# Half a batch's projections, squares, roots and unit vectors moved within the last rounds of FFN 1

## The reference, cut to what matters

```
x = x + 0.5 * ffn(layernorm(x))            # FFN 1: hidden 384, silu(gate) * up, down
x = x + attention(layernorm(x))            # attention: x + gate * out @ Wo
x = x + 0.5 * ffn(layernorm(x))            # FFN 2

# attention(x):
h = rmsnorm(x) * norm_w
q = l2norm(h @ Wq)    # 4 heads of 32
k = l2norm(h @ Wk)    # 2 heads of 32
v = h @ Wv
out = softmax(causal(q @ k.T * exp(log_temperature))) @ v
```

## Time and profile before

| | us |
|---|---|
| median of 3 runs | 430.47 (430.47 to 430.57) |
| profiled execution | 430.8 |
| its span | 429.0 |
| PE busy | 393.1 (92%) |
| ACT busy | 370.0 (86%) |
| DVE busy | 349.1 (81%) |
| POOL busy | 299.7 (70%) |
| granted clock of TensorE, mean | 0.999 |

### The profile page before, as it was taken

The page is one execution under the profiler, slowest core; times in us unless marked ns, Lnnn a source line. Parts: engine busy times, 40 slices in busy tenths (PEclk is TensorE's granted clock), DMA queues, the critical chain, the costliest instruction groups (busy, mean ns, idle before and its releaser), DMA issues.

```text
span 429.0 us, 13351 instructions
## 1 busy us (share of the span) xinstructions
PE 393.1 (92%) x5403; PEld 219.8 (51%) x5403; DVE 349.1 (81%) x887; ACT 370.0 (86%) x497; POOL 299.7 (70%) x381
## 2 busy tenths in 40 slices
PE   0689999898898899999999999999999999999994
PEld 0346666574444434635546446456354346765754
DVE  4889999689596997997998979968769848878554
ACT  4799999776797698999998998999987989999950
POOL 5689999985799858857758578581123658999850
PEclk9999999999999999999999999999999999999999
DMA  6487523513605706418237148055142225566532
GB/s 171 102 194 156 67 49 50 99 27 76 124 2 76 125 2 127 74 16 143 46 75 101 26 76 128 2 107 93 20 87 46 39 38 75 111 136 100 126 96 79
DMA packets 119233, 35.25 MB, mean 82 GB/s; under 512 B 101632, under 2 KB 119168, under 8 KB 119168
## 3 DMA queue, kind: packets, MB, share of 16 engines
q1 hardware_dynamic: 117888, 34.02, 43.1%
q10 hardware_dynamic: 1280, 0.33, 0.3%
HBM read 4.98 MB, written 4.19 MB: 21 GB/s over the span
## 4 chain that ended last, share of the span: by engine, by line
PE 55%; DVE 13%; ACT 10%; DMA 8%; issue 6%; POOL 6%; SPq 1%; DVEq 0%; ACTq 0%
PE ps L740 11%; PE ps L770 10%; PE ps L777 10%; PE ps L511 9%; DMA QKT<-ST 5%; ACT XN L463 3%; PE ps L804 3%; PE ps L575 3%; PE ps L564 3%; DVE H L332 3%; ACT PT L884 3%; PE ps L600 3%; DVE RD L245 2%; PE ps L747 2%; DMA XT<-w_int 2%
## 5 line engine op out<-in xcount | busy, mean ns | idle before, releaser
L884 ACT ACTIVATE PT<-ps,k_exp 128x1024 f32<-128x1024 f32 x144 | 153.9, 1122 | 14.1 <-PE ps L747 8.0
L511 PE MATMUL ps<-XT,WT 128*128 128x512 f16 x384 | 93.9, 383 | 6.2 <-DVE H L332 2.0
L740 PE MATMUL ps<-QKT 128*32 128x512 f16 (+1 forms) x1280 | 86.6, 359 | 5.0 <-DMA QKT<-ST 3.3
L770 PE MATMUL ps<-PT,V 128*32 128x512 f32 (+3 forms) x768 | 76.1, 486 | 0.0
L777 PE MATMUL ps<-PT,ones 128*32 128x512 f32 (+3 forms) x768 | 76.1, 486 | 0.0
L438 POOL TENSOR_TENSOR HL<-H,HH 128x1024 f16<-128x1024 f32 x31 | 66.6, 2148 | 8.3 <-ACT HH L487 5.3
L332 DVE SCALAR_TENSOR_TENSOR H<-SG,k_isilu,ps 128x1536 f32<-128x1536 f32 x32 | 57.9, 1808 | 13.9 <-ACT SG L481 6.3
L511 PEld LDWEIGHTS ps<-XT,WT 128*128 128x128 f16 x384 | 34.5, 98 | 50.6 <-issue 10.5
L463 ACT ACTIVATE XN<-X,NB,RS 128x128 f32<-128x128 f32 x128 | 52.5, 483 | 2.5 <-POOL NB L410 2.5
L481 ACT ACTIVATE SG<-ps,k_silu 128x1536 f32<-128x1536 f32 x32 | 48.8, 1526 | 4.4 <-DVE H L332 4.3
L740 PEld LDWEIGHTS ps<-QKT 128*32 128x32 f16 x1280 | 31.0, 96 | 41.2 <-issue 16.0
(11 more groups left out here) (140 smaller groups left out, 664.3 us busy)
## 6 DMA issues: line engine op xcount, KB each, us to landing
result<-X SPq DMA_DIRECT2D x15, 256.0 KB, 2.5
X<-in_L_attn_x SPq DMA_DIRECT2D x7, 512.0 KB, 4.6
X<-in_L_attn_x SPq DMA_DIRECT2D x2, 256.0 KB, 4.7
XT<-w_int SPq DMA_TRANSPOSE x32, 3.1
QKT<-ST SPq DMA_TRANSPOSE x18, 5.8
AXT<-AS SPq DMA_TRANSPOSE x16, 3.0
w_int<-in_L_ffn_w_gate SPq DMA_DIRECT2D x1, 192.0 KB, 4.0
w_int<-in_L_ffn_w_up SPq DMA_DIRECT2D x1, 192.0 KB, 4.7
```

Of the source, the lines that this page charges most:

```text
L511: i = e.matmul(out[:, j, :], WT[:, wp, w * NJ + j, :], XT[k % 2][:, xp, :], start=a == 0, stop=a == len(passes) - 1)
L740: i_ = e.matmul(dst[r, :].rearrange("p (s a n) -> p s a n", a=2, n=P), QKT[k % 2][:, i // TPC, NH + hp, key0 + r.start:key0 + r.stop], q.r ...
L770: e.matmul(sums_of(h, 0, n), V[k % 2][:, i, v0:v0 + HD], weights_of(g, h, o, n), start=i == 0, stop=i >= TPC * qc, skip_group_check=True)
L884: e.activation(dst, SCORES[(SLOT0[g] + i) % 2][:, :, :], ACT.Exp, scale=k_exp[:, 0:1]).then_inc(a_exp, 1)
```

## The change: what it does

TensorE: the second part of half 0's projection moves from the end of round 12 to the middle of round 12, half 1's first part from the end of round 13 to the end of round 12, its second part from the end of round 14 to the middle of round 13. ScalarE, VectorE and GpSimdE follow: `x_lo` of both halves goes from GpSimdE to VectorE, behind `normalise(1)` and `stats(2)`; `x_hi` of both goes ahead of H's remainder in its round; all three root rounds of half 0 stand in round 13; its unit vectors go to GpSimdE, behind round 13; `stack_hi(0)` and `stack_hi2(0)` go from round 15 to 14, where the sums of half 1 also go; three parts of `rstds` move together behind round 12 on GpSimdE. SP's list stays.

```diff
@@ att_pool: GpSimdE
             def x_lo(m, half):
-                if isinstance(m, int) and m < 2:
-                    e.wait_ge(a_xh0, m + 1)
-                else:
-                    e.wait_ge(a_xh, m - 1)
+                e.wait_ge(a_xh, m - 1)
...
+            def first_unit(m, half):
+
+                e.wait_ge(a_inv, 10)
+                e.tensor_tensor(
+                    QN[half][:, :, :, :],
+                    V[0][:, half * TPC:half * TPC + TPC, 0:DQ + DK].rearrange("p t (h d) -> p t h d", d=HD),
+                    R[half][:, :, :].unsqueeze(3).to_broadcast([P, TPC, NQK, HD]), ALU.mult)\
+                    .then_inc(a_qn, 1)
@@ att_dve: VectorE
+            def x_lo(m):
+                e.wait_ge(a_xh0, m + 1)
+                e.tensor_tensor(AS[m][:, 1, :, :], AN[m][:, :, :], AS[m][:, 0, :, :],
+                                ALU.subtract).then_inc(a_xl, 1)
+
             if first == "sums":
                 sums(0, 0)
-                norms(0, 2, 0, 1, (0, 2))
-                return
-            if first == "unit":
-                norms(0, 2, 0, 1, (2, 3))
-                unit(0, 10, 0, 0)
+                norms(0, 2, 0, 1)
                 return
             if first == "stack":
                 stack_hi2(0, 0)
+                sums(1, 1)
                 return
             if first == "second":
 
-                sums(1, 1)
                 norms(10, 4, 1, 2)
                 unit(0, 20, 1, 1)
...
                     {"stats": stats, "normalise": normalise}[what](m, m, m, *part)
+                    if what == "normalise" and m:
+                        x_lo(0)
+                    if (what, m) == ("stats", 2):
+                        x_lo(1)
@@ gpsimd: after, then between
             ffn_pool(e, 0, None, {-1: down_weights,
-                                  9: first(("x_hi", 0), ("x_lo", 0)), 10: first(("x_hi", 1), ("x_lo", 1)),
-                                  11: first(("rstds_a", 2)), 14: first(("stack_lo", 0)),
-                                  15: first(("rstds_b", 3))},
-                     {13: first(("rstds_b", 2), ("rstds_a", 3))})
+                                  12: first(("rstds_a", 2), ("rstds_b", 2), ("rstds_a", 3)),
+                                  13: first(("unit", 0))},
+                     {9: first(("x_hi", 0)), 10: first(("x_hi", 1)), 14: first(("stack_lo", 0)),
+                      15: first(("rstds_b", 3))})
@@ scalar: between, then after
             ffn_act(e, 0, None, {0: lambda: ffn_act(e, 0, [("silu", 1)]),
-                                 13: first(("v_out", 0, 0), ("v_out", 0, 1), ("squares", 0)),
-                                 14: first(("v_out", 1, 0)),
-                                 15: first(("stack_hi", 0), ("v_out", 1, 1), ("squares", 1))})
+                                 12: first(("v_out", 0, 0)),
+                                 13: first(("v_out", 1, 0)),
+                                 14: first(("v_out", 1, 1), ("squares", 1), ("stack_hi", 0))},
+                    {12: first(("v_out", 0, 1), ("squares", 0))})
@@ vector: between
-                     13: stage("sums"), 14: stage("unit"), 15: stage("stack")})
+                     13: stage("sums"), 14: stage("stack")})
@@ tensor: after, then between
-                ffn_pe(e, 0, has_low, None, {11: first_projection(0, 0), 12: first_projection(0, 1),
-                                             13: first_projection(1, 0), 14: first_projection(1, 1)})
+                ffn_pe(e, 0, has_low, None, {11: first_projection(0, 0), 12: first_projection(1, 0)}, None,
+                       {12: first_projection(0, 1), 13: first_projection(1, 1)})
```

More of the change, by code:

```diff
@@ L454, in ffn_pool, with ffn_act @@
             pipeline(e, [(3, x_lo), (0, amid), (0, h_lo), (5, rstd_pair)], early, after)
-        def ffn_act(e, ph, only=None, between={}):
+        def ffn_act(e, ph, only=None, between={}, after={}):
             def normalise(k, c):
@@ L501, in ffn_act, with ffn_pe @@
                          (0, h_hi)],
-                     early)
-        def ffn_pe(e, ph, low, only=None, after={}, banks_read=None):
+                     early, after)
+        def ffn_pe(e, ph, low, only=None, after={}, banks_read=None, between={}):
             def products(k, w, out, bank_free=lambda j: None):
@@ L578, in down_of, with amid @@
                 i.then_inc(s_dn, 1)
+            def amid(k, c):
+                if k in between:
+                    between[k]()
             def last_wo(k, c):
@@ L594, in ffn_pe @@
             early = [(gate_, 0)] if ph else [(gate_, 0), (up, 0)]
-            pipeline(e, [(1, gate_), (-1, down), (0, last_wo), (1, up)], early, after, True, 0 if ph else 2)
+            pipeline(e, [(1, gate_), (0, amid), (-1, down), (0, last_wo), (1, up)], early, after, True,
+                     0 if ph else 2)
         def project(e, dst, ts=range(TPC)):
@@ L1019, in stack_lo @@
                                 ST[half][:, NH:NQK, :, 0, :], ALU.subtract).then_inc(a_lo, 1)
+            def first_unit(m, half):
[5 more added lines that the diff above has]
+                    .then_inc(a_qn, 1)
             if first is not None:
-                {"rstds_a": rstds_a, "rstds_b": rstds_b, "x_hi": first_x_hi, "x_lo": x_lo,
+                {"rstds_a": rstds_a, "rstds_b": rstds_b, "x_hi": first_x_hi, "unit": first_unit,
                  "stack_lo": stack_lo}[first[0]](first[1], first[1])
```

## The result

The changed kernel takes 435.08 us (median of 4 runs, 434.49 to 436.16) against 430.52 for the kernel before on the same chip (430.47 to 430.68). The ratio is 1.0106, 95% interval 1.0094 to 1.0118: 4.6 us slower, where 434.4 was forecast. The profiled execution is the longest of the four, 436.16.

The account below looks back on a forecast made before the run. Bound: handoffs among VectorE, ScalarE and GpSimdE, about 75 to 112 us, not matmuls. Half 1's unit vectors +3.9 on 430.8 gave 434.7 profiled, less 0.3 for the median: 434.4; own range 433.6 to 435.2, with rivals 431.6 to 436.6.

Parts of the forecast that it names:

- two holds: GpSimdE's L438 holds VectorE's half 0 roots in round 13 (`hidden(14)` +2.2), then scaling L1099 in round 14 (`hidden(15)` +4.3).
- Rival A: Round 14: scaling L1099 gets in ahead of L438 of chunk 14, one hold, not two; +2.3, 432.8; chance 0.15.
- C: TensorE, idle from 95.5 to 99.2, slows to 1.2 GHz: up to +2.5 on the forecast, 436.9; chance 0.08.
- third hold: Round 15: L438 of chunk 15 meets half 1's roots at 101.9, pushing them to 104.1 to 106.1; unit vectors +3.9.
- Rival B: Round 13: L438 of chunk 13 comes after the roots; faster or equal, -0.7 to +0.1, say 430.1; chance 0.20.
- The test that I had named: Whole kernel before 84 us: the forecast is also wrong if anything there moves by more than 0.7.

Follow-up runs that it names:

- TensorE filled: The changed kernel with 14 filling matmuls on TensorE behind the up products of chunk 15: 434.77 us, ratio 1.0096.

## Why the prediction was right

The forecast case was that two holds and a third meeting move the unit vectors of half 1 by 3.9, giving 434.4; measured 435.1 and 435.3. The holds are shown by undoing them. That the number is this near is partly luck: the sum had 0.8 too much at the unit vectors, and nothing for TensorE's slow products. Step by step:

1. **L438 of chunk 13 in the middle of the roots: right.** Forecast 88.3 with the rest held until 90.4; measured 88.10 and 90.27. One instruction more was done than I had: a round and its follower's first.
2. **`hidden(14)` and `hidden(15)`: right in cause, 0.6 and 0.8 too late.** Forecast 92.3 and 99.05, measured 91.72 and 98.24. L438 ended 0.17 sooner than in the sum, and behind it came four instructions of the roots where the sum had six (one more was done ahead, and the held one ended with L438 itself): that makes the first difference, and GpSimdE's shorter unit vectors add the second.
3. **The scaling held: right.** 1.76 us, forecast 1.75. Rival A, one hold only, needed it at 0.24. Undoing the sums' place alone put `hidden(15)` at 96.25 and left 1.0034.
4. **GpSimdE's unit vectors: 1.48, forecast 1.65.** They ended at 92.7, not at 93.4. The Trainium skill's page "GPSIMD Engine Reference", section "Performance versus the Vector engine", gave an estimate of 1.69 in proportion; all traces with L1027 show 1.48, and the measurement decides.
5. **The stack: half right.** Unit vectors of half 1 at 105.35, +3.1 and not +3.9, in the profiled execution; with TensorE filled 104.98. Yet in the first profile the first exponentials came 5.9 later and the fourth group's scores 4.7, not 3.9: what bounded both was TensorE, whose filling began at 106.70 and not at 104.55. With TensorE filled the exponentials started at 106.72 with no wait for TensorE, +2.75 like the unit vectors, so the path through them that the forecast named holds where the clock stays up.
6. **The clock: wrong as a chance, right in place.** I had seen the idle stretch (95.5 to 99.2; measured 95.27 to 98.46) and gave C only 0.08, with "filling matmuls stand just there" against it. They stand behind the down products of two chunks, and those ran at half speed first. All eight runs of the changed kernel have a mean clock of 0.986 to 0.993, where 44 of the 45 later runs of the kernel before have 0.996 or more. C gave up to 2.5 on top; the profiled execution lies 1.5 above the one with TensorE filled. Forecast and C were not rivals: the first makes the idle time that the second needs. The median is 0.7 above the forecast, near the upper end of its own range of 433.6 to 435.2; that the clock makes this difference isn't shown, since the filled kernel is at 434.77 and the intervals overlap.

The third hold, forecast at full length, was seen in full only where the clock stayed up (2.00 with TensorE filled, 2.00 with the unit vectors first), at 0.43 and 1.30 in the two profiles of the changed kernel. Held roots and slow down products take the same place, so their prices don't add.

Rival B, faster or equal, had its point of decision right: L438 of chunk 13 must come after the roots. With a wait that makes it so, the kernel with x's remainder on VectorE gives 0.9978. The whole change with the unit vectors and L438 behind the roots still gives 1.0061, though, where B had 430.1 (L438 starts there at 90.90, not at B's 89.6). B overlooked that the scaling would be held (1.76) and that the roots would then meet the last L438 (2.00).

x's remainders took 0.68 and 0.80 on VectorE, forecast 0.65, and cost nothing where they stand. The test that I had named, nothing before 84 us moved by more than 0.7, failed: `hidden(12)` and the residual and the statistics beside it came 0.9 sooner (GpSimdE's own L438 of chunk 11 even 2.3). Of the 0.9, every row up to 66 us had 0.3 already; the rest is near the 0.65 of the forecast. It is the gain of the shorter GpSimdE queue, which TensorE's first wait shows (1.11, now 0.50), and as forecast it wasn't kept.

What GpSimdE's small instruction does was a term in itself: L999, 1.00 us from 87.13, lay beside VectorE's rounds from 87.38, at 0.18 each. The Trainium skill's page "SBUF — State Buffer", section "Who interferes with whom", would have them wait to its end at 88.13. The trace disagrees for these 4 elements and agrees for L438's 1024.

## What to carry to other kernels

Where VectorE has a chain of small SBUF instructions, look for the long GpSimdE instruction that will start inside it, and place that by an explicit wait on the chain's own semaphore; beside reductions and instructions that read PSUM it costs nothing (the reduction 0.94 and `hidden` 1.80 beside L438, as without it). Taking work off an engine moves all that is queued behind it, so the shorter queue can collide where the longer one did not: here one constant wait turned +0.3% into -0.2%. When a forecast itself leaves TensorE idle for longer than it was anywhere nearby, the lower clock can follow from it (it did in all eight runs of the changed kernel) and belongs with a price in its sum or range, not among the rivals.

## What was not expected of the hardware

A 24-element instruction was held for 2.16 us when L438 started in the same hundredth (87.97): which of the two issued first can't be read, but VectorE's got nowhere until GpSimdE's had ended, at 90.10. The granted clock fell to 0.50 behind 3.19 us of idle TensorE in both profiles of the changed kernel and stayed there for about 10 and 7 us, as its windows give it, while it stood at 1.00 behind 2.74 us in another order, though that kernel's other runs show it lower in two of six.
